# Activation codes turned as 16-bit halves, and the whole of attention's first score pass beside layer 1's tail, in a four-layer kernel on one core

## Chip, core and metric

One core of a Trainium2 chip runs one fixed program. The metric is device time in microseconds (us) of one execution, taken as the median of the runs. TensorE is called PE in the profile, VectorE DVE, ScalarE ACT, GpSimd POOL, and SyncE (which issues the DMAs) SP.

## What is computed

Eight batches of 512 tokens by 256 features pass through four layers, with modulations made from a conditioning vector. Layer 0 is a gated recurrence and an MLP whose activations are rounded to 8-bit codes before every product; layer 1 blends a style in and has a gelu MLP; layer 2 is attention with 16 heads; layer 3 a state-space layer and an MLP. Cut to the two parts that the change touches:

```python
# layer 0: every linear step, 7 products with wi, wf, wg, wo, wm1 (two halves), wm2
def _act_quant(x):
    scale = 127.0 / clip(max(abs(x), axis=-1), 1e-05)
    return clip(round(x * scale), -128, 127) / scale
def _bitlinear(x, w, nw):
    xn = x * rsqrt(mean(square(x), -1) + 1e-08) * nw
    return _act_quant(xn) @ _weight_quant(w).T

# layer 2: q, k, v of 16 heads of 16 features, with rotary positions
attn = einsum('bhnd,bhmd->bhnm', q, k) * scale
attn = softmax(attn, axis=-1)
out = einsum('bhnm,bhmd->bhnd', attn, v)
```

## The kernel before

The tokens of a batch lie in T = 4 tiles of 128 (one token per partition). All products need the features on the partitions, so tiles are turned on PE through an identity matrix (`turn`, L94) into PSUM and copied from there by ACT or DVE. PSUM has eight banks of 128 x 512 float32.

The program has three blocks of time. A setup runs to about 85 us. The block `layers01` runs layers 0 and 1 over the eight batches to 887.72 us in the profiled execution, where all engines meet; then `layers23` runs attention in rounds, and at its end layer 3.

The order within `layers01` is written by hand. Each engine has a table (`PE_TURN`, `DVE_TURN`, `ACT_TURN`, `POOL_TURN`, `SP_TURN`) of steps (stage, tile, batches ahead), which is gone through once per batch, so that up to five batches are in work at once. A second set of tables (`PE_BESIDE` and so on) hangs steps of attention's batch 0 behind named steps of the last batches of layer 1; B - 1 is the last batch. What stands in those tables is left out of the tables of attention. An engine executes its list strictly in order; signals (semaphores) between engines say when an item may start.

**Codes of layer 0.** ACT multiplies a tile by its scale and adds ROUND = 12582912.0, so that float32 rounding leaves the integer code in the lowest bits of the number: stages `xq` (L1167, three tiles of 256 features per token tile), `xoq` (L1190), `xq2` (L1198), `hq` (L1215). PE turns the float32 values through `ident`: 24, 8, 8 and 32 turns of 128 x 128 in a batch, 72 in all. DVE reads the bank, subtracts ROUND and writes bf16: `qT` (L1523, 128 x 768 over two banks), `qoT` (L1553, 128 x 256), `qT2` (L1594, 128 x 512), `qhT` (L1621, 128 x 512). The 768 columns of `xq` fill bank 0 and half of bank 1. Bank 1 is also read by ACT's gate step (L1175, signal `sg_ready`), so `xq` of a tile waits for that of the tile before. The products follow as `proj` (L88).

**Scores of attention.** A score pass over one batch has 64 rows (16 heads x 4 query tiles): PE computes a 128 x 512 row (stage `s`, L2158), DVE takes its maximum (L2194). After 16 rows the maxima of four heads are split into three bf16 parts (`npart`, L2201 to L2205), turned on PE (`nturn`, L94), copied (`nkeep`, L2210) and laid by three DMAs of SP (L1941) into three extra rows of q. The matching rows of k hold ones, which POOL sets by a memset of 3 x 8192 (L1957, step `ones`). The second score pass (`st`, L2035) then gives scores less their maximum, for ACT to exponentiate (L1983), and `pv` (L2044) multiplies by v. From batch 1 on, q and k are copied early by ACT (L2018) and laid out by 24 DMAs of SP (L1935, `dup`); the first score row of a batch waits for all of them.

Of batch 0, rows 0 to 47 stand beside the end of layer 1, over banks 0 and 1, two or three rows behind each `f1` or `f2` step (the gelu MLP's products, L88 and L1461); rows 48 to 63 stand in the middle of attention's first round. PE issues row n once DVE has reduced row n - 2.

Of the kernel before, what the change touches and what calls it, by code (L numbers as in the profile page):

```python
# [618 lines left out]
SP_BESIDE = ((("dup", 0, 0), ("dup", 1, 0), ("nkeep", 0, 0)), (("nkeep", 1, 0),))  # L619
# [39 lines left out]
    ("f1", 5, B - 1): (("s", 21, 0), ("s", 22, 0)),
    ("f1", 6, B - 1): (("s", 23, 0), ("s", 24, 0), ("s", 25, 0)),  # L660
    ("f1", 7, B - 1): (("s", 26, 0), ("s", 27, 0)),
    ("f2", 0, B - 1): (("s", 28, 0), ("s", 29, 0), ("s", 30, 0)),
    ("f2", 1, B - 1): (("s", 31, 0), ("s", 32, 0)),
    ("f2", 2, B - 1): (("s", 33, 0), ("s", 34, 0), ("s", 35, 0)),
    ("f2", 3, B - 1): (("s", 36, 0), ("s", 37, 0), ("nturn", 1, 0)),
    ("f2", 4, B - 1): (("s", 38, 0), ("s", 39, 0), ("s", 40, 0)),
    ("f2", 5, B - 1): (("s", 41, 0), ("s", 42, 0)),
# [2092 lines left out]
```

## Time and profile before

| | us |
|---|---|
| runs | 1993.22, 1990.77, 1985.62 |
| median | 1990.77 |
| the profiled execution | 1985.53 |
| its span (first to last instruction of the profile) | 1983.7 |
| PE busy in the span | 1747.9 (88%) |
| DVE busy | 1359.0 (69%) |
| ACT busy | 1106.3 (56%) |
| POOL busy | 615.3 (31%) |

The profiled execution is 1.8 us longer than its span. "Busy" counts an engine while one of its instructions runs; matmuls overlap, so pitches (start to start) say more about PE than durations. PEclk is the clock granted to PE as a share of full speed, 2.4 GHz; the lower level is 1.2 GHz. A time in a list of instructions is the start, then the duration of the whole group, with the count behind it. Text in brackets is how long the engine had been idle, and what it waited for.

### The profile page before, as it was taken

How to read it: one execution, taken by the hardware profiler on the slowest of the kernel's cores; microseconds unless marked ns; L12 is line 12 of the kernel's file. 1: busy time of each engine (PE TensorE's matmuls, PEld its weight loads, DVE VectorE, ACT ScalarE, POOL GpSimd, SP SyncE). 2: the span in 40 equal slices, each digit the busy share in tenths (PEclk: the TensorE clock that was granted, in tenths of full speed). 3: DMA queues.
4: the chain of work that ended last, by engine and by line, in shares of the span. 5: the costliest groups of instructions: out<-in, count | busy, mean ns of one | idle time of the engine just before them, and what ended most of it. 6: DMA issues, size and time to landing. Idle time of an engine off the chain costs nothing.

```text
span 1983.7 us, 25674 instructions
## 1 busy us (share of the span) xinstructions
PE 1747.9 (88%) x8444; PEld 1046.9 (53%) x8463; DVE 1359.0 (69%) x2873; ACT 1106.3 (56%) x2117; POOL 615.3 (31%) x874
## 2 busy tenths in 40 slices
PE   1367677989999999878989999999999998999998
PEld 1145455667667657543344444454545444666666
DVE  5755888888887765567867686877686734566650
ACT  6634667868867753314675757566666664322221
POOL 0145556756754633620000001010101012334342
PEclk9756788999999999988999999999999999999999
DMA  9440000000000002303030303030303005000000
GB/s 373 123 158 1 10 19 20 12 9 19 14 1 14 20 4 65 65 17 64 5 67 5 67 5 67 5 67 4 67 4 67 4 4 149 3 11 22 11 22 21
DMA packets 94422, 83.57 MB, mean 42 GB/s; under 512 B 9881, under 2 KB 87842, under 8 KB 94034
## 3 DMA queue, kind: packets, MB, share of 16 engines
q1 hardware_dynamic: 94192, 81.91, 15.1%
q8 instruction: 68, 1.11, 0.2%
q14 instruction: 64, 0.52, 0.1%
q10 hardware_dynamic: 98, 0.03, 0.0%
HBM read 51.26 MB, written 5.09 MB: 28 GB/s over the span
## 4 chain that ended last, share of the span: by engine, by line
PE 40%; DVE 8%; ACT 6%; issue 1%; POOL 0%; POOLq 0%; DVEq 0%; ACTq 0%
PE k_psum L88 13%; PE k_psum L2518 6%; PE k_psum L2044 5%; PE k_psum L2105 5%; PE k_psum L2158 5%; PE k_psum L2035 4%; PE k_psum L94 3%; DVE l_small L2194 2%; ACT l_prob L1983 1%; ACT L1983 1%; ACT L1999 1%; ACT l_gu L1999 1%; DVE l_xn L2267 1%; DVE l_small L2181 1%; DVE l_xn L2269 1%
## 5 line engine op out<-in xcount | busy, mean ns | idle before, releaser
L2194 DVE TENSOR_REDUCE l_small<-k_psum 128x1 f32<-128x512 f32 x512 | 329.7, 685 | 134.9 <-PE k_psum L2158 131.5
L1983 ACT ACTIVATE l_prob<-k_psum 128x512 f32<-128x512 f32 x512 | 286.4, 596 | 184.5 <-PE k_psum L2035 181.3
L1971 POOL TENSOR_TENSOR k_x_res<-k_x_res,k_arena_a 128x256 f32<-128x256 f32 x32 | 23.2, 726 | 418.5 <-DVE k_arena_a L2238 418.5
L2044 PE MATMUL k_psum<-l_prob,l_v 128*32 128x512 f32 x1024 | 138.1, 612 | 0.2
L2105 PE MATMUL k_psum<-k_arena_a,l_gu 128*128 128x256 f32 x512 | 135.6, 394 | 0.7 <-ACT l_gu L1999 0.7
L88 PE MATMUL k_psum<-l_turned_over,k_arena_a 128*128 128x512 f32 x256 | 120.8, 596 | 4.2 <-ACT l_gu L1999 4.2
L88 PE MATMUL k_psum<-k_arena_b,l_w_f 128*128 128x512 f32 x256 | 122.0, 604 | 0.0
L1461 PE MATMUL k_psum<-l_w_f,k_arena_b 128*128 128x256 f32 x512 | 120.4, 380 | 0.2 <-ACT k_arena_b L1274 0.2
L88 PE MATMUL k_psum<-l_hT,k_arena_b 128*128 128x512 f32 x256 | 114.3, 593 | 0.0
L2518 PE MATMUL k_psum<-k_arena_b,l_gu 128*128 128x256 f32 x512 | 113.0, 379 | 0.0
L2105 PEld LDWEIGHTS k_psum<-k_arena_a,l_gu 128*128 128x128 f32 x512 | 98.1, 198 | 19.7 <-issue 2.2
L2463 ACT ACTIVATE l_gu<-k_psum,k_arena_c 128x512 f32<-128x512 f32 x64 | 44.0, 687 | 112.3 <-PE k_psum L88 112.3
L2518 PEld LDWEIGHTS k_psum<-k_arena_b,l_gu 128*128 128x128 f32 x512 | 96.9, 190 | 16.1 <-issue 3.8
L2158 PE MATMUL k_psum<-l_kT,l_qT 96*128 96x512 bf16 x256 | 90.8, 397 | 15.7 <-DVE l_small L2194 14.2
L1461 PEld LDWEIGHTS k_psum<-l_w_f,k_arena_b 128*128 128x128 f32 x512 | 94.4, 190 | 13.3 <-ACT k_arena_b L1274 0.7
L2035 PE MATMUL k_psum<-l_qT,l_kT 99*128 99x512 bf16 x256 | 88.6, 391 | 12.6 <-PEq L2702 5.9
L2035 PE MATMUL k_psum<-k_arena_b 99*128 99x512 bf16 x256 | 87.4, 385 | 10.2 <-ACT l_prob L1983 9.2
L88 PE MATMUL k_psum<-k_t_wm,l_qT 128*128 128x512 bf16 x237 | 75.3, 420 | 22.9 <-DVE k_arena_a L1601 13.9
L2158 PE MATMUL k_psum<-k_arena_b 96*128 96x512 bf16 x256 | 90.8, 394 | 3.2 <-DVE l_small L2194 1.6
L94 PE MATMUL k_psum<-k_ident,k_arena_a 128*128 128x128 f32 x451 | 71.0, 296 | 24.4 <-ACT k_arena_c L1175 14.8
L88 PE MATMUL k_psum<-k_arena_a,l_xT 128*128 128x512 f32 (+1 forms) x256 | 89.4, 493 | 0.4 <-DVE l_xn L2255 0.4
L2579 DVE TENSOR_TENSOR l_add<-k_psum,k_arena_c 128x256 f32<-128x256 f32 x32 | 13.6, 424 | 96.7 <-PE k_psum L2518 96.7
(389 smaller groups left out, 3873.4 us busy)
## 6 DMA issues: line engine op xcount, KB each, us to landing
su_raw<-in_L_cond_wa SPq DMA_DIRECT2D x6, 1536.0 KB, 21.8
k_arena_b<-k_arena_c SPq DMA_DIRECT2D x32, 192.0 KB, 3.5
k_x_res<-in_x SPq DMA_DIRECT2D x1, 4096.0 KB, 19.9
k_arena_b<-k_arena_c SPq DMA_DIRECT2D x32, 128.0 KB, 3.2
out<-k_x_res SPq DMA_DIRECT2D x8, 512.0 KB, 2.9
l_mod_mlp<-mod SPq DMA_DIRECT2D x8, 384.0 KB, 3.6
l_qT<-k_arena_c SPq DMA_DIRECT2D x16, 192.0 KB, 3.6
l_kT<-k_arena_c SPq DMA_DIRECT2D x16, 192.0 KB, 3.3
```

Of the source, the lines that this page charges most:

```text
L88: last = nc.tensor.matmul(out, w, m, start=(i == 0), stop=(i == len(pairs) - 1), **kw)
L94: return nc.tensor.matmul(out, in_, ident, is_transpose=True, start=True, stop=True)
L1461: last = pe.matmul(psum[:, 6 + i % 2, 0:D], gu[:, f, tok(i)], w_f2[:, f, :], start=(f == 0), stop=(f == KF - 1))
L1983: act.activation(prob[:, s % 2, j, :], psum[:, 2 + n % 2, :], ACT.Exp, scale=float(HD) ** -0.5).then_inc(exp_ready.sem, 1)
L1999: act.activation(gu[:, n, :], psum[:, 5 + n % 2, :], ACT.Gelu).then_inc(gu_ready.sem, 1)
L2035: pe.matmul(psum[:, 2 + n % 2, :], kT[e % 2][:, head, tok(s % T)], qT[e % 2][:, head, :], start=True, stop=True).then_inc(st_ready.sem, 1)
L2044: last = pe.matmul(psum[j * BLOCK:(j + 1) * BLOCK, 4, :], v[e % 2][:, kt, at:at + BLOCK], prob[:, n % 2, j, :], start=(kt == 0), stop=(kt ...
L2105: last = pe.matmul(psum[:, mlp_bank(e, t), 0:D], gu[:, f, tok(t)], w_2[:, f, :], start=(f == 0), stop=(f == KF - 1))
L2158: pe.matmul(psum[:, n % 2, :], qT[e % 2][0:SROWS, n // T, tok(n % T)], kT[e % 2][0:SROWS, n // T, :], start=True, stop=True).then_inc(s_re ...
L2194: dve.tensor_reduce(mx[:, n % T, n // T:n // T + 1], psum[:, n % 2, :], AX.X, ALU.max).then_inc(max_ready.sem, 1)
L2463: act.activation(gu[:, n, :], psum[:, n % 2, :], ACT.Gelu_apprx_tanh, bias=b_1[:, n:n + 1]).then_inc(gu_ready.sem, 1)
L2518: last = pe.matmul(psum[:, 2 + n % 2, 0:D], gu[:, f, tok(n)], w_2[:, f, :], start=(f == 0), stop=(f == KF - 1))
```

## The change

1. **Codes as halves.** ACT adds ROUND + 0x4380 (17280) in place of ROUND, so the lower 16 bits of the float32 number are themselves a valid, positive bf16 pattern. PE turns only these lower halves, as bf16 values with a step of two elements, through the upper halves of `ident` (also with a step of two), and writes bf16 into the bank. DVE reads them as unsigned 16-bit integers and subtracts 17280. All 72 turns of a batch change. The 768 columns of `xq` now fit bank 0, and its wait for `sg_ready` goes.
2. **Scores.** All 64 rows of batch 0 and all four groups of maxima stand beside the end of layer 1, over banks 0, 1 and 4: up to four rows behind each step. PE issues row n of batch 0 once row n - 3 is reduced. SP issues the DMAs of groups 2 and 3 before the block's end.
3. **Ones.** Those of batch 0 are written by ACT (an exponential with scale 0 over 3 x 8192) behind the last gelu step. Those of batch 1 are cut into eight memsets of POOL.

```diff
+MIDDLE = 0x4380
-    ("s5p", 4, B - 1): (("ones", 0, 0),),
+    ("gelu", 7, B - 1): (("ones", 0, 0),)}
-SP_BESIDE = ((("dup", 0, 0), ("dup", 1, 0), ("nkeep", 0, 0)), (("nkeep", 1, 0),))
+SP_BESIDE = ((("dup", 0, 0), ("dup", 1, 0), ("nkeep", 0, 0)), (("nkeep", 1, 0), ("nkeep", 2, 0), ("nkeep", 3, 0)))
 # PE_BESIDE, two of its lines
-    ("f1", 2, B - 1): (("s", 13, 0), ("s", 14, 0), ("s", 15, 0)),
+    ("f1", 2, B - 1): (("s", 19, 0), ("s", 20, 0), ("s", 21, 0), ("s", 22, 0)),
...
+        def low(a, cols):
+            return a.bitcast(BF16).rearrange("p (n a) -> p n a", a=2)[:, cols, 0]
+        identh = ident[:].bitcast(BF16).rearrange("p (n a) -> p n a", a=2)[:, :, 1]
+        def halves(a):
+            return psum[:, a, :].bitcast(BF16)
+        def codes(a):
+            return psum[:, a, :].bitcast(U16)
...
-   last = ac.activation(xw[:, t, j, :], xw[:, t, j, :], ACT.Copy, bias=ROUND, scale=qs[e % 2][:, t, j:j + 1])
+   last = ac.activation(xw[:, t, j, :], xw[:, t, j, :], ACT.Copy, bias=ROUND + MIDDLE, scale=qs[e % 2][:, t, j:j + 1])
...
                             pe.wait_ge(qT_ready.sem, qT_ready.at(e, t))
-                            pe.wait_ge(sg_ready.sem, sg_ready.at(e, t))
...
-   last = turn(nc, two_banks(0)[:, tok(j)], xw[:, t, j // KD, tok(j % KD)], ident[:])
+   last = turn(nc, halves(0)[:, tok(j)], low(xw[:, t, j // KD, :], tok(j % KD)), identh[:])
...
-   V.tensor_scalar(qT[...], two_banks(0)[:, 0:3 * D], ROUND, None, ALU.subtract)
+   V.tensor_scalar(qT[...], codes(0)[:, 0:3 * D], float(MIDDLE), None, ALU.subtract)
    # xoq/qoT, xq2/qT2 and hq/qhT in the same way
...
+    def banks_of(e, n):
+        return (0, 1) if e else (0, 1, 4)
+    def s_bank(e, n):
+        return banks_of(e, n)[n % len(banks_of(e, n))]
     def max_bank(e, n):
-        return 5 if e == 0 and n < 2 else 7
+        return 7 if e else 5
...
-                if n >= 2:
-                    pe.wait_ge(max_ready.sem, max_ready.at(e, n - 1))
+                if n >= len(banks_of(e, n)):
+                    pe.wait_ge(max_ready.sem, max_ready.at(e, n - len(banks_of(e, n)) + 1))
...
-                if e:
-                    pool_chain.link(nc.gpsimd.memset(v[1][:], 1.0))
-                nc.gpsimd.memset(kT[e][SROWS:SROWS + MROWS, :, :], 1.0).then_inc(ones_ready, 1)
+                pool_chain.link(nc.gpsimd.memset(v[1][:], 1.0))
+                for h in range(0, HEADS, 2):
+                    nc.gpsimd.memset(kT[1][SROWS:SROWS + MROWS, h:h + 2, :], 1.0).then_inc(ones_ready, 1)
...
+            if stage == "ones":
+                act.activation(kT[0][SROWS:SROWS + MROWS, :, :].rearrange("p h n -> p (h n)"),
+                               ident[SROWS:SROWS + MROWS, 0:1].to_broadcast([MROWS, HEADS * L]),
+                               ACT.Exp, scale=0.0).then_inc(ones_ready, 1)
```

**PE, steps f1 2 to f1 5 of layer 1's last batch.** L88 on `k_arena_b,l_w_f` is an f1 step, L2158 the score rows, L94 on `l_npart` a turn of maxima. Before:

```order
L88 MATMUL k_psum<-k_arena_b,l_w_f 128x512 x2
L2158 MATMUL k_psum<-l_kT,l_qT 128x512 x3
L88 MATMUL k_psum<-k_arena_b,l_w_f 128x512 x2
L2158 MATMUL k_psum<-l_kT,l_qT 128x512 x2
L88 MATMUL k_psum<-k_arena_b,l_w_f 128x512 x2
L2158 MATMUL k_psum<-l_kT,l_qT 128x512 x3
L94 MATMUL k_psum<-l_identb,l_npart 12x128 x4
```

Now (the score rows are L2181, the products L91, the turns L97):

```order
L91 MATMUL k_psum<-k_arena_b,l_w_f 128x512 x2
L2181 MATMUL k_psum<-l_kT,l_qT 128x512 x4
L97 MATMUL k_psum<-l_identb,l_npart 12x128 x4
L91 MATMUL k_psum<-k_arena_b,l_w_f 128x512 x2
L2181 MATMUL k_psum<-l_kT,l_qT 128x512 x4
```

Each step is followed by four rows, and the first turn of maxima stands one step earlier.

**PE, the middle of attention's first round.** L2158 on `l_kT,l_qT` are rows 48 to 63 of batch 0, L2158 on `k_arena_b` the rows of batch 1, L2035 and L2044 the second pass and its product with v. Before:

```order
L94 MATMUL k_psum<-l_identb,l_part 96x128 x8
L2035 MATMUL k_psum<-l_qT,l_kT 128x512 x2
L2158 MATMUL k_psum<-l_kT,l_qT 128x512 x10
L2044 MATMUL k_psum<-l_prob,l_v 32x512 x4
L2158 MATMUL k_psum<-l_kT,l_qT 128x512
L2035 MATMUL k_psum<-l_qT,l_kT 128x512
L2158 MATMUL k_psum<-l_kT,l_qT 128x512 x5
L2035 MATMUL k_psum<-l_qT,l_kT 128x512 x2
L2158 MATMUL k_psum<-k_arena_b 128x512 x2
```

Now:

```order
L97 MATMUL k_psum<-l_identb,l_part 96x128 x8
L2058 MATMUL k_psum<-l_qT,l_kT 128x512 x2
L2067 MATMUL k_psum<-l_prob,l_v 32x512 x4
L2058 MATMUL k_psum<-l_qT,l_kT 128x512 x3
L2181 MATMUL k_psum<-k_arena_b 128x512 x2
```

The sixteen rows are gone from here, and the first rows of batch 1 stand right behind the last turns of q and k.

**ACT, the end of the block.** The last gelu steps are L1274, and L1983 is attention's exponential. Before:

```order
L1274 ACTIVATE k_arena_b<-k_psum,l_small 128x512 x8
L867 UNCONDITIONAL_BRANCH
L2606 UNCONDITIONAL_BRANCH
L1983 ACT_TABLE_LOAD
L1983 ACTIVATE l_prob<-k_psum 128x512
```

Now:

```order
L1287 ACTIVATE k_arena_b<-k_psum,l_small 128x512 x8
L1998 ACT_TABLE_LOAD
L1998 ACTIVATE l_kT<-k_ident 3x8192
L880 UNCONDITIONAL_BRANCH
L2631 UNCONDITIONAL_BRANCH
L2006 ACTIVATE l_prob<-k_psum 128x512
```

The ones stand in front of the block's end, and with them the load of the exponential's table.

## Rows read from the trace of the kernel before

**Rows 1.** All engines by stretch: start:end, length, busy (count), PEclk, DMA share, GB/s
```profile
95.00:232.00 137.00, 84.48 (x355) 57.40 (x356) 82.15 (x173) 61.70 (x172) 69.61 (x95) 0.61 0.21 69
232.00:350.00 118.00, 87.73 (x484) 64.33 (x486) 101.42 (x211) 83.17 (x218) 70.67 (x97) 0.83 0.06 17
...
524.00:610.00 86.00, 82.45 (x458) 60.36 (x460) 74.03 (x151) 68.24 (x165) 50.42 (x68) 0.98 0.03 9
...
820.00:888.00 68.00, 49.72 (x181) 28.06 (x180) 47.04 (x85) 5.78 (x9) 26.71 (x39) 0.92 0.03 12
```

**Rows 2.** PE's longest wait from 524 to 610: total us, times, longest
```profile
PE k_psum L88 <- DVE k_arena_a L1601: 2.0, 2, 1.1
```

**Rows 3.** PE's turns by group, 350 to 820: shapes, count, busy us, mean ns
```profile
L94 PE MATMUL k_psum<-k_ident,k_arena_a 128*128 128x128 f32 x288 | 40.5, 273 | 1.9 <-ACT k_arena_c L1175 1.4 <-DVE l_add L1627 0.5
L94 PE MATMUL k_psum<-k_ident,k_arena_c 128*128 128x128 f32 x112 | 17.7, 273 | 0.1
```

**Rows 4.** PE in order of time: float32 turns, then bf16 turns (start, duration)
```profile
744.21 0.60 PE L94 MATMUL k_psum<-k_ident,k_arena_a 128*128 128x128 f32 x4
744.64 0.60 PE L94 MATMUL k_psum<-k_ident,l_xn 128*128 128x128 f32 x4
...
779.46 0.61 PE L94 MATMUL k_psum<-l_identb,l_part 128*96 128x128 bf16 x8
```

**Rows 5.** DVE by group: reading codes (350 to 820), bf16 maxima (830 to 888)
```profile
L1621 DVE TENSOR_SCALAR l_qhT<-k_psum 128x512 bf16<-128x512 f32 x48 | 32.2, 684 | 4.3 <-PE k_psum L94 4.3
...
L1523 DVE TENSOR_SCALAR l_qT<-k_psum 128x768 bf16<-128x768 f32 x16 | 15.3, 954 | 12.9 <-PE k_psum L94 12.9
...
L2210 DVE COPY k_max_rows<-k_psum 12x512 bf16<-12x512 bf16 x2 | 0.8, 401 | 0.0
```

**Rows 6.** PE, and one row of DVE, in order of time, layer 0 of batch 0
```profile
120.60 1.52 PE L94 MATMUL k_psum<-k_ident,k_arena_a 128*128 128x128 f32 x6 [1.39 <-ACT k_arena_c L1175]
...
126.02 1.51 PE L94 MATMUL k_psum<-k_ident,k_arena_a 128*128 128x128 f32 x6 [1.38 <-ACT k_arena_c L1175]
...
122.15 0.96 DVE L1523 TENSOR_SCALAR l_qT<-k_psum 128x768 bf16<-128x768 f32 x1 [1.14 <-PE k_psum L94]
```

**Rows 7.** PE's wait for the gate step, 232 to 350
```profile
PE k_psum L94 <- ACT k_arena_c L1175: 4.7, 4, 2.3
```

**Rows 8.** PE in order of time, the end of layer 1, and DVE's last row there
```profile
828.62 1.88 PE L88 MATMUL k_psum<-k_arena_b,l_w_f 128*128 128x512 f32 x4
...
831.50 0.39 PE L2158 MATMUL k_psum<-l_kT,l_qT 96*128 96x512 bf16 x1 [0.57 <-DVE l_small L2194]
831.73 1.88 PE L88 MATMUL k_psum<-k_arena_b,l_w_f 128*128 128x512 f32 x4
...
847.65 1.21 PE L2158 MATMUL k_psum<-l_kT,l_qT 96*128 96x512 bf16 x2 [6.62 <-DVE l_small L2194]
...
881.40 0.60 PE L2158 MATMUL k_psum<-l_kT,l_qT 96*128 96x512 bf16 x2
...
884.77 1.38 DVE L2189 TENSOR_SCALAR l_xn<-k_x_res,l_small 128x256 f32<-128x256 f32 x4
```

**Rows 9.** POOL, then DVE, in order of time, at the ones of batch 0
```profile
837.87 6.92 POOL L1957 MEMSET l_kT<- 3x8192 bf16 x1
...
837.94 6.88 DVE L2201 TENSOR_SCALAR l_npart<-l_small 128x16 bf16<-128x16 f32 x1
```

**Rows 10.** ACT in order of time, its first instruction of attention
```profile
887.72 1.28 ACT L1983 ACT_TABLE_LOAD   x1 [28.09 <-PEq L2702]
```

**Rows 11.** PE in order of time, the middle of attention's first round
```profile
921.01 0.60 PE L2158 MATMUL k_psum<-l_kT,l_qT 96*128 96x512 bf16 x2 [0.52 <-ACT k_arena_c L2018]
...
934.49 1.01 PE L2158 MATMUL k_psum<-k_arena_b 96*128 96x512 bf16 x2
```

**Rows 12.** SP's queue in order of time, and DMA busy tenths, 905 to 935 in 40 slices
```profile
910.02 19.20 SPq L1935 DMA_DIRECT2D k_arena_b<-k_arena_c  x24
...
DMA  0000000048889998737975087999998898810000
```

More of the change, by code:

```diff
@@ L17 @@
 BF16 = mybir.dt.bfloat16
+U16 = mybir.dt.uint16
 B, L, D = 8, 512, 256
@@ L659 @@
[L659 to L667, printed above, removed]
@@ L670 @@
+    ("f2", 1, B - 1): (("s", 47, 0), ("s", 48, 0), ("s", 49, 0), ("s", 50, 0)),
+    ("f2", 2, B - 1): (("s", 51, 0), ("s", 52, 0), ("s", 53, 0), ("s", 54, 0)),
+    ("f2", 3, B - 1): (("s", 55, 0), ("s", 56, 0), ("s", 57, 0), ("s", 58, 0), ("nturn", 2, 0)),
+    ("f2", 4, B - 1): (("s", 59, 0), ("s", 60, 0), ("s", 61, 0), ("s", 62, 0)),
+    ("f2", 5, B - 1): (("s", 63, 0),),
+    ("f2", 7, B - 1): (("nturn", 3, 0),)}
 DVE_BESIDE = {
@@ L1321, in _ @@
                         for k in range(KD):
-                            last = turn(nc, psum[:, t % 2, tok(k)], xo[:, t, tok(k)], ident[:])
+                            last = turn(nc, halves(t % 2)[:, tok(k)], low(xo[:, t, :], tok(k)), identh[:])
                         last.then_inc(xo_turned.sem, 1)
@@ L1337, in _ @@
                             for k in range(KD):
-                                last = turn(nc, psum[:, 4 + t, tok(KD * i + k)], mx2[:, 2 * t + i, tok(k)], ident[:])
+                                last = turn(nc, halves(4 + t)[:, tok(KD * i + k)], low(mx2[:, 2 * t + i, :], tok(k)), identh[:])
                         last.then_inc(turned2.sem, 1)
@@ L1355, in _ @@
                         for k in range(T):
-                            last = turn(nc, psum[:, 4 + (3 * i + c) % 2, tok(k)], h[:, i, tok(c * T + k)], ident[:])
+                            last = turn(nc, halves(4 + (3 * i + c) % 2)[:, tok(k)], low(h[:, i, :], tok(c * T + k)), identh[:])
                         last.then_inc(h_turned.sem, 1)
@@ L2164, in pe @@
                     pe.wait_ge(nT_ready.sem, nT_ready.at(e, n))
-                front = e + 1 if n == NG - 1 else e
+                front = e + 1 if n == NG - 1 and e else e
                 pe.wait_ge(v_ready.sem, v_ready.at(min(front, B - 1), T))
-                if n == 2 and e + 1 < B:
+                if n == 2 and 0 < e < B - 1:
                     pe.wait_ge(xT_ready.sem, xT_ready.at(e + 1, KD))
@@ L2587, in turns @@
         for b in range(B + 1):
-            yield from attention_order(b)
+            for item in attention_order(b):
+                if item not in EARLY2:
+                    yield item
     def late(table):
```

69 lines of the change are left out of this document (36 added, 33 removed).

## The prediction

> **What bounds the kernel now.** I read the stretches first, then who waits for whom in each. In the steady part of layers 0 and 1 PE is busy 82.45 of 86 us at a clock of 0.98, DVE 74.03, ACT 68.24, POOL 50.42 [rows 1]; the longest sum of PE's waits there is 2.0 us [rows 2]. PE sets the pace, and DVE is not far behind. From 95 to 232 no engine is busy for more than 85 of 137 us and PE's clock is 0.61: chains of steps set the time, and each wait on them counts whole. From 232 to 350 DVE is the busiest, 101.42 of 118, and PE waits 4.7 us for the gate step [rows 1, 7]. At the end of layer 1 the score rows run through PE and DVE together, PE busy 49.72 and DVE 47.04 of 68: a slot of two f1 products and three rows takes 831.73 - 828.62 = 3.11 us, because the third row waits 0.57 for the reduction that frees its bank, and one stall of 6.62 stands in it [rows 1, 8]. From 888 on, attention's rounds follow one another; the change shortens only the first of them.
>
> **PE's turns, steady part.** Four float32 turns take 744.64 - 744.21 = 0.43 us from start to next start, about 109 ns each. From first start to last end the four take 0.60, and eight bf16 turns 0.61 [rows 4]: half as long each, about 55 ns. If a turn of halves goes like bf16, it saves 53 ns. From 350 to 820 the 288 turns of `k_arena_a` are codes (`xq`, `hq`), and 16 of every 24 of `k_arena_c` are (`xoq` and `xq2`, beside 8 plain ones), 75 of 112 [rows 3]: 363 in all, and 576 - 363 = 213 before 350. 363 x 53 ns = 19.2 us. The bf16 rows read packed values, and nothing in the trace reads every second one, so the saving lies between 0 (a read of 16 bits in 32 goes like float32, the 109 ns row) and 53; below 0 it would go only if the step cost more than the float32 that fills the same bytes, for which no row speaks. I take 53, since these are bf16 matmuls of the same shape but for the step. Of 19.2 I keep 16.5: PE has 3.55 us of slack in 86 now, and with 3.8 less work a batch the chains through DVE and ACT are waited for a little more often.
>
> The Trainium skill ("SBUF — State Buffer", on its cachelines) says that a step is free as long as at least two accesses fall into a 16-byte line, up to 8 bf16 elements; a step of two lies inside that. By it the saving is the 53 ns; by the pessimistic end it is nothing. No run here has shown it yet.
>
> **DVE's readings.** 128 x 512 float32 takes 684 ns and 128 x 768 takes 954; a bf16 copy of 512 columns out of PSUM takes 401 [rows 5]. A reading of 16-bit integers lies between 401 and 684. I take 410 for 512 columns and 540 for 768, nearest to the bf16 copy. That is about 5 us per batch off DVE (8 readings of `hq` at 0.27, 4 of `xq` at 0.41, 2 of `xq2`, 4 of `xoq` at 0.14). In the steady part this is off the path and worth nothing by itself, but it keeps DVE behind PE: 74.03 less 5.8 in 86 is 68.2, against PE's 82.45 less 4.4 = 78.0. It matters where the chains are bare, at the start.
>
> The Trainium skill ("VectorE: DVE Perf Modes", Why PSUM operands drop a tier) puts a PSUM operand at most at the double rate, and float32 from PSUM at the single; with the row of 401 ns the trace agrees for bf16. If subtraction from integers stayed at the single rate, the start would give 3.3 us less (8 tiles x 0.41).
>
> **The start, 95 to 350.** In batch 0 a tile takes 126.02 - 120.60 = 5.42 us: the gate wait 1.38, six turns at the half clock, the reading, the product. The gate wait goes, the turns lose 6 x 107 = 0.64 (half clock, twice 53), the reading 0.41: 2.4 us, if PE alone decided. But DVE waits only 1.14 per tile [rows 6] and does its list in order, so a tile can shrink by about 1.14 + 0.41 = 1.5. With the first tile not gaining the wait, batch 0 gives about 4.9. In batch 1 the tiles are also held by ACT's and POOL's chain of the batch ahead; I take 1.9, and 0.5 for the other turns up to 232. From 232 to 350 some 140 turns are worth 140 x 53 = 7.4 and the gate waits 4.7 [rows 7], together 12 at the most; DVE, the busiest there, loses about 7 of its 101. I take 5, with 2 and 9 as ends. Start in all: 12.3, between 6 and 18.
>
> **The end of layer 1.** Four rows over three banks: three go out at once, the fourth waits for one reduction, as the third of three does over two banks, so I price the slot again at 3.11 us. Without its wait a slot of three rows takes 3.11 - 0.57 = 2.5, with two rows 0.39 less, 2.2. From 820.0, where the first row starts: 2.2, 3 slots of three rows at 2.5 (three banks, no wait), 13 of four at 3.11, then 2.0 + 1.8 + 1.8 for the last three steps and 1.8 for the turns of maxima and three of layer 1's own: 57.5, so the last f2 ends at 877.5 where it now ends near 881.4 [rows 8]. The 6.62 stall came from POOL's memset of 6.92 us, beside which one small DVE instruction took 6.88 [rows 9]; it is gone, and pays for the sixteen rows that are added. Its follow-on, a step at the half clock, goes too. Behind it now stand DVE's last steps to 886.15 and the engines' meeting, 1.6 to 887.72 [rows 8, 10]. After, the meeting waits for three DMA issues of SP instead (19.20 / 24 = 0.8 each, rows 12), 2.4, since nturn 3 and its copy run beside DVE's last steps: 877.5 + 2.4 + 1.6 = 881.5 in place of 887.72, **6.2 us**, with 3 (the issues start only once DVE has done everything) and 8 as ends. The ones on ACT: POOL writes the same 3 x 8192 in 6.92 us [rows 9], and even at twice that they are hidden, as ACT idles 28.09 us there [rows 10]. If that cover were gone, they would cost their 7 to 14 us whole. The 1.28 of the table load moves under the same cover, though round 0's turns wait for other things as well, so I count nothing for it.
>
> **The first round.** Sixteen rows leave the middle, from 921.01 to about 933.4 [rows 11]. But what follows them, the first row of batch 1, needs all 24 `dup` DMAs: SP issues them until 910.02 + 19.20 = 929.22, and the queues are busy up to slice 35 of 40, about 932 [rows 12]. So a wait for DMA takes the place of the rows, and of 13 us at the most I count 934.49 - 932.4 = **2.1**, with 0 and 3.3 (the last issue at 929.22 plus 2) as ends; no row shows when the last of the 24 lands, only that the queues are empty then. The memset of batch 1 in eight pieces costs seven more instruction starts, which ACT's copy of v waits for; I charge 0.3 as an estimate, 0 to 1 as ends.
>
> **The sum.** 12.3 + 16.5 + 6.2 + 2.1 - 0.3 = 36.8 us. From the profiled execution, 1985.53 - 36.8 = 1948.7. The median of the runs stands 5.2 above that execution, and from it the sum gives 1954.0. I predict between them, **1952**.
>
> **The rivals.**
> (a) *The step costs what float32 costs.* PE's 16.5 goes, and about 4 at the start (1.3 in batch 0 where DVE decides, the rest from 232 to 350); gate wait, DVE, the end and the first round stay: 36.8 - 20.5 = 16.3; from 1988.2, midway between the two starting points, about 1972. For it: the bytes passed over are the same. Against: the bf16 rows. By the page on SBUF it would not happen.
> (b) *Another engine becomes the bound.* ACT at 68.24 and DVE at 68.2 of 86 are in chains with PE; if only half of PE's 19.2 arrives, and half of the 12.3: 36.8 - 6.9 - 6.1 = 23.8, about 1964.
> (c) *More arrives than I count* (all of 19.2, 16 at the start): 43.2, about 1945.
> (d) *Slower: PE's clock falls.* From 232 to 350, with the same steps but more waits, the granted clock is 0.83, against 0.98 [rows 1]. If shorter turns open enough gaps that the steady part runs at 0.83 too, PE's 78.0 us in 86 become 78.0 x 0.98 / 0.83 = 92.1, 6.1 more than 86; over the 470 us from 350 to 820 that is +33, where +16.5 of gain was counted: the sum is 36.8 - 16.5 - 33 = -12.7, about 2001. It decides where the steady part loses the 20.3 that the rest gains, 3.7 us in 86: 78.0 x 0.98 / 89.7, a clock of 0.85. Against it: PE would still be busy nine tenths of the time.
> (e) *The halves are not read faster by DVE either*: 3.3 less, 1955; inside the forecast's own range.
>
> **Chances.** Forecast with (e), 1945 to 1960: 0.58. (a) 0.14, (b) 0.16, (c) 0.08, (d) 0.04. The range leaves out (d) and the outer part of (c) and (a): **1938 to 1973**. A measurement of this kernel can tell about 0.5% (10 us) from no change; the forecast, (a), (b) and (c) lie beyond that, (a) least clearly. Faster 0.93, same 0.04, slower 0.03.
>
> **What would show it.** In the profile after: eight turns of codes in about 0.45 us (if four take 0.43, (a)); readings at 410 and 540 ns; tiles of batch 0 at 3.9 us and no wait for L1175's successor; PEclk above 0.95 from 350 on (else (d)); slots of 3.1 us at the end of layer 1 with no stall over 1 us, and 61.5 us (now 67.7) from the first score row to attention's start; PE waiting for a DMA, 8 us or so, before batch 1's first row, with that row only 2 us nearer to the round's start. Wrong it would be above all if the turns' 53 ns is not there, or if that DMA wait is longer than the rows it replaces.

## The result, and the profile after

The changed kernel took 1970.95 us in the median of four runs (1969.29 to 1973.95), beside 1991.99 for the kernel before (its three runs and a fourth of 1993.38): a ratio of 0.9902, with a 95% interval of 0.9877 to 0.9928. Over all ten executions of it (six more stood in the last series of experiments) the median is 1969.6. The profiled execution took 1969.29 us, 16.2 less than that of before. The prediction's 1952 was 19 us too low: faster, as forecast, by about half of what was forecast.

The stretches of the kernel after (start:end, length, busy and count of PE, PEld, DVE, ACT, POOL, PEclk, DMA share, GB/s), which answer to [rows 1]:

```profile
232.00:350.00 118.00, 82.54 (x482) 56.98 (x481) 94.31 (x206) 83.20 (x226) 73.82 (x99) 0.84 0.05 17
...
524.00:610.00 86.00, 81.67 (x458) 59.80 (x457) 61.12 (x135) 67.06 (x165) 52.02 (x72) 0.94 0.05 16
...
820.00:888.00 68.00, 53.21 (x203) 28.08 (x203) 46.39 (x104) 19.89 (x21) 16.52 (x22) 0.92 0.04 13
```

DVE is down from 74.03 to 61.12 busy in the same 86 us, but PE's clock there is 0.94 and no longer 0.98. That stretch shows more of the fall than the steady part as a whole, where the clock went from 0.97 to 0.96. The whole of it from 350 to 820, after and then before:

```profile
350.00:820.00 470.00, 446.70 (x2322) 311.16 (x2320) 327.28 (x718) 317.18 (x732) 261.82 (x407) 0.96 0.09 24
350.00:820.00 470.00, 449.41 (x2286) 321.62 (x2300) 352.60 (x715) 323.07 (x750) 256.50 (x390) 0.97 0.09 24
```

PE's longest waits from 524 to 610 (total, times, longest), which answer to [rows 2]:

```profile
PE k_psum L97 <- ACT l_xn L1253: 2.9, 1, 2.9
PE k_psum L91 <- DVE k_arena_a L1613: 1.1, 2, 0.9
```

A wait for the first `xn` of layer 1, which is 0.6 us long before, has grown to 2.9. The line of before, in the same stretch:

```profile
548.43 0.66 PE L94 MATMUL k_psum<-k_ident,l_xn 128*128 128x128 f32 x4 [0.61 <-ACT l_xn L1240]
```

The operations themselves came out as priced. PE in order of time, six turns of codes; then DVE's readings from 350 to 820 by group:

```profile
533.28 0.51 PE L97 MATMUL k_psum<-k_ident,k_arena_a 128*128 128x128 bf16 x6
533.63 1.94 PE L1473 MATMUL k_psum<-l_w_f,k_arena_b 128*128 128x256 f32 x8
```

```profile
L1633 DVE TENSOR_SCALAR l_qhT<-k_psum 128x512 bf16<-128x512 uint16 x48 | 19.4, 417 | 4.1 <-PE k_psum L97 4.1
L1535 DVE TENSOR_SCALAR l_qT<-k_psum 128x768 bf16<-128x768 uint16 x16 | 8.8, 552 | 13.8 <-PE k_psum L97 13.8
```

Six turns in 533.63 - 533.28 = 0.35 us are 58 ns each (109 before, 56 forecast), so reading every second 16-bit element costs PE next to nothing (packed bf16: about 55). The readings take 417 and 552 ns (forecast 410 and 540).

Where the 16.2 us came from, by marks that both traces have:

| mark | before | after | gained so far |
|---|---|---|---|
| first xn of layer 1 turned | 255.74 | 248.01 | 7.7 |
| turn of layer 1's second norm (`yn`), batch 1 | 387.59 | 377.24 | 10.4 |
| first xn of layer 1 turned, two batches on | 399.50 | 390.95 | 8.6 |
| first score row | 820.03 | 806.58 | 13.5 |
| start of attention (turn of its first xn) | 888.29 | 872.67 | 15.6 |
| first score row of batch 1 | 934.49 | 918.33 | 16.2 |
| end | 1983.7 | 1967.5 | 16.2 |

The end of layer 1 gave 2.2 (forecast 6.2) and the first round 0.5 (1.8). How the rest is shared depends on the mark: with the mark in front of the steady part's first long wait for `xn` the start has 10.4 (forecast 12.3) and the steady part 3.1 (16.5); with the mark just behind that wait it is 8.6 and 4.9. Either way twelve to thirteen of the twenty missing microseconds are in the steady part. These are two single executions, and the start scatters by itself: the first `xn` begins on ACT at 252.4 to 257.9 us in the four traces with float32 turns, and at 245.0 to 250.0 in the eleven with the turns, waits and POOL order of after up to there.

### The profile page after: what moved, and what is told of

The parts are those of the page before. It is cut to its first block, busy times and chain, and to the rows that moved or that the text cites. A ratio compares the mean times of both kernels' runs of the same rounds, so it can differ in the third digit from the quotient of the medians.

```text
span 1967.5 us, 25698 instructions
## 1 busy us (share of the span) xinstructions
PE 1719.6 (87%) x8463; PEld 1017.9 (52%) x8463; DVE 1310.6 (67%) x2873; ACT 1112.7 (57%) x2118; POOL 611.8 (31%) x880
## 4 chain that ended last, share of the span: by engine, by line
PE 40%; DVE 8%; ACT 6%; issue 1%; SPq 0%; DMA 0%; POOL 0%; POOLq 0%; DVEq 0%; ACTq 0%
PE k_psum L91 13%; PE k_psum L2541 6%; PE k_psum L2067 5%; PE k_psum L2128 5%; PE k_psum L2181 4%; PE k_psum L2058 4%; PE k_psum L97 3%; ACT l_prob L2006 1%; DVE l_small L2217 1%; ACT L2006 1%; ACT L2022 1%; ACT l_gu L2022 1%; DVE l_xn L2290 1%; DVE l_small L2204 1%; DVE l_xn L2292 1%
## 5 line engine op out<-in xcount | busy, mean ns | idle before, releaser
L91 PE MATMUL k_psum<-l_turned_over,k_arena_a 128*128 128x512 f32 x256 | 120.9, 596 | 4.2 <-ACT l_gu L2022 4.2
L91 PE MATMUL k_psum<-k_arena_b,l_w_f 128*128 128x512 f32 x256 | 120.4, 597 | 0.0
L91 PE MATMUL k_psum<-l_hT,k_arena_b 128*128 128x512 f32 x256 | 114.3, 592 | 0.0
L2181 PE MATMUL k_psum<-k_arena_b 96*128 96x512 bf16 x256 | 90.5, 393 | 8.6 <-DMA k_arena_b<-k_arena_c 5.7
L91 PE MATMUL k_psum<-k_t_wm,l_qT 128*128 128x512 bf16 x256 | 81.6, 432 | 17.4 <-DVE k_arena_a L1613 10.6
L2181 PE MATMUL k_psum<-l_kT,l_qT 96*128 96x512 bf16 x256 | 86.5, 387 | 8.3 <-DVE l_small L2217 7.0
L91 PE MATMUL k_psum<-k_arena_a,l_xT 128*128 128x512 f32 (+1 forms) x256 | 92.5, 506 | 0.4 <-DVE l_xn L2278 0.4
L2602 DVE TENSOR_TENSOR l_add<-k_psum,k_arena_c 128x256 f32<-128x256 f32 x32 | 13.5, 423 | 96.6 <-PE k_psum L2541 96.6
L1219 ACT ACTIVATE k_arena_a<-k_psum,l_small 128x512 f32<-128x512 f32 x64 | 43.9, 686 | 55.7 <-PE k_psum L91 55.6
```

The lines of the kernel that those rows point to most:

```text
L91: last = nc.tensor.matmul(out, w, m, start=(i == 0), stop=(i == len(pairs) - 1), **kw)
L1219: ac.activation(h[:, t // 2, t % 2 * 512:(t % 2 + 1) * 512], psum[:, 4, :], ACT.Silu, scale=deq2[:, t // 2:t // 2 + 1]).then_inc(sgate_rea ...
L2181: pe.matmul(psum[:, s_bank(e, n), :], qT[e % 2][0:SROWS, n // T, tok(n % T)], kT[e % 2][0:SROWS, n // T, :], start=True, stop=True).then_i ...
```

## Experiments

### Each half of the change alone

`x1_codes` is the kernel before with the codes as halves and nothing else; `x2_scores` the kernel after with the codes as float32, over two banks and with the wait for the gate step.

```diff
# x1_codes, against before: every hunk of part 1 of the change, as
-   turn(nc, psum[:, t % 2, tok(k)], xo[:, t, tok(k)], ident[:])
+   turn(nc, halves(t % 2)[:, tok(k)], low(xo[:, t, :], tok(k)), identh[:])
```

> The kernel before with the codes turned as halves and nothing else of the change. Theory T1 (from the traces of before and after): in the steady part the stretch of a batch from the first xoq to the first xn of layer 1 lasts as long as ACT's and POOL's in-order lists (22.7 us before, 23.0 after), so the 50 of 72 turns that lie in it save nothing; about 10.4 us are won up to 350 and 3 in the steady part, so 13 us in all, 1972 to 1975 in the profiled execution. Rival T2 (the halves take the steady part's saving back through PE's clock, wherever the turns lie) gives the same total, but then PE's wait for xn stays under 1 us a batch. Rival T3 (the score part costs something that hides the codes' gain): this kernel gains 25 or more.

> The kernel after with the codes turned as float32, through two banks and with the wait for the gate step, as before; the score part of the change stays. The traces give 2.2 us at the end of layer 1 and 0.5 in attention's first round: 2 to 3 us less than before, 1983. If the parts help or hinder each other (T3), it is not the complement of the kernel with codes alone: then faster by 6 or more, or slower.

Measured: `x1_codes` 1972.32 us (ratio to before 0.9937, 0.9916 to 0.9957), `x2_scores` 1986.07 (0.9998, 0.9984 to 1.0012). The codes carry most of the gain: 14.9 us between the medians of that series, where the whole change has 19 to 21 in other series, and the intervals of the two ratios overlap. The score part can't be told from nothing in the runs (1 us between the medians, 2 to 3 expected); its trace shows the same 2.2 us at layer 1's end as the whole change (68.26 from the first score row to attention's start before, 66.06 here, 66.09 after). T3 falls. PE waits 2.9 us and more for `xn`, as T1 says and not under 1 us, T2's sign. But what T2 says of the clock is there as well: from 350 to 800 the half-clock stretches add up to 44.4 us in `x1_codes`, 37.5 in after, and 27.3 before.

### Is it PE that paces the stretch before xn?

`x3_root3` changes the order on POOL alone. `x5_pe` and `x7_pe3` make the turns of `xq` two and three times from batch 3 on, `x9_before_pe` makes them twice in the kernel before. (T4, in two of the expectations, is the theory that PE's long wait for `xn` is followed by stretches at the half clock, which cost more than extra turns do.)

```diff
# x3_root3, against after (POOL_TURN)
-    ("x2", 2, 2), ("xb", 1, 0), ("xb", 2, 0), ("root2", 0, 3), ("x2", 3, 2), ("mx", 3, 5), ("root3", 0, 2), ("sgn", 0, 4), ("xb", 3, 0),
+    ("x2", 2, 2), ("xb", 1, 0), ("root2", 0, 3), ("x2", 3, 2), ("root3", 0, 2), ("xb", 2, 0), ("mx", 3, 5), ("sgn", 0, 4), ("xb", 3, 0),
# x5_pe, against after (x7_pe3: the first range twice; x9_before_pe: the same line of before)
-                        for j in range(3 * KD):
+                        for j in [*range(3 * KD if e >= 3 else 0), *range(3 * KD)]:
```

> The kernel after with one change of order on POOL: root3 (which the first xn of layer 1 waits for) ahead of xb 2 and mx 3, and root2 ahead of xb 2. If T1 holds, xn starts 1 to 2 us earlier in each batch and PE's wait of 2.9 for it shrinks by as much: 4 to 5 batches in the steady part, so 5 to 9 us less than after, and a steady period of 72 us in place of 73.5. If PE's own work or its clock is the bound (T2), the period stays within 0.3 us and the time within 2.

> The kernel after with each of the 24 turns of xq made twice from batch 3 on (the second overwrites the first with the same values): 24 x 56 ns = 1.3 us more PE work a batch, nearly all inside the stretch that T1 says PE doesn't pace. T1: PE's wait for xn falls from 2.9 to about 1.6 us and the period doesn't change, within 0.3 us (under 2 us in all). T2: the period grows by 1.3 us, 6 to 7 us in all over five batches.

> The kernel after with the turns of xq made three times from batch 3 on: 2.6 us more PE work a batch. T4: PE's wait for xn goes to about 0.5 us, the half clock stands only behind the 32 one-column products, and the period is 72.3 to 73 us (the extra work is still covered by the stretch that ACT and POOL pace): 1957 to 1962. If more PE work simply costs its time: 6.5 us above the kernel with the turns made twice, 1965.

> A control: the kernel before with its 24 float32 turns of xq made twice from batch 3 on, 2.6 us more PE work a batch. Before has only 0.6 us of wait for xn to fill, so if what counts is the wait that is filled (T4), this is slower by about 2 us a batch, 8 to 10 us in all. If extra turns help by themselves, wherever they stand, it is faster than before.

Measured: `x3_root3` 1971.19 us, no better than after, where T1 expected 5 to 9 less and T2 no change; `x5_pe` 1958.69 in one run, twelve less than after although it only adds work, which neither theory expected; `x7_pe3` 1969.60 in one, above both figures of its expectation; `x9_before_pe` 1993.33 in one, against 1986.5 for before beside it, 6.8 slower where 8 to 10 were expected. Single runs decide little here, since one kernel scatters by ten to twelve us (below). To read them I took from each trace, for the three batches from 365 to 590, how long it is from ACT's first `xoq` to its first `xn`, and how long to the next `xoq`:

| kernel | xoq to xn, us | turns of codes in it | whole period, us | PE's wait at xn |
|---|---|---|---|---|
| before | 22.7, 22.8, 22.7 | 50 | 74.7, 74.3, 73.4 | 0.6 |
| x9_before_pe | 22.9, 22.9, 22.9 | 56 | 74.9, 74.7, 74.4 | 0.0 |
| after | 23.2, 23.0, 23.0 | 50 | 74.4, 73.3, 74.8 | 3.0, 2.9, 2.9 |
| x1_codes | 23.2, 23.0, 23.0 | 50 | 76.1, 75.1, 75.1 | 3.0, 2.9, 2.9 |
| x5_pe | 22.6, 22.6, 22.6 | 68 | 72.4, 72.3, 72.3 | 1.8 |
| x7_pe3 | 22.6, 22.6, 22.6 | 86 | 72.8, 74.8, 72.8 | 0.9 to 1.0 |
| x3_root3 | 20.6, 20.6, 20.6 | 50 | 74.9, 74.9, 74.6 | 0.5 |

Fifty of a batch's 72 turns of codes stand between these marks, and the stretch is as long with 50 bf16 turns as with 86, or with 50 in float32. PE does not pace it: of what those 50 save (50 x 53 ns = 2.65 us), 2.3 comes back as the wait at `xn`, which goes from 0.6 to 2.9. What does pace it is shown by `x3_root3`: with root3 earlier on POOL the stretch is 2.4 us shorter. POOL in order of time, kernel after, and ACT's `xn` behind it:

```profile
458.67 0.72 POOL L1053 TENSOR_TENSOR k_x_res<-k_x_res,l_add 128x256 f32<-128x256 f32 x1
459.35 0.72 POOL L1001 TENSOR_TENSOR k_arena_c<-k_arena_c,l_mod_norm 128x256 f32<-128x256 f32 x1
460.15 0.73 POOL L1002 TENSOR_TENSOR k_arena_c<-k_arena_c,l_mod_norm 128x256 f32<-128x256 f32 x1
460.97 0.20 POOL L978 TENSOR_SCALAR l_small<-l_small 128x4 f32<-128x4 f32 x1
461.25 1.60 POOL L979 TENSOR_TENSOR l_small<-l_small 128x4 f32<-128x4 f32 x1
...
462.88 0.51 ACT L1253 ACTIVATE l_xn<-k_x_res,l_small 128x256 f32<-128x256 f32 x1 [1.07 <-POOL l_small L979]
```

root3 is L978 and L979; the two instructions of `mx` (L1001, L1002) stand in front of it. But the batch is not shorter in `x3_root3`. The wait has only moved on by one link, from `xn` to the copy of `xT` on ACT. PE in order of time there:

```profile
464.18 0.66 PE L97 MATMUL k_psum<-k_ident,l_xn 128*128 128x128 f32 x4 [0.48 <-ACT l_xn L1253]
...
469.37 0.63 PE L97 MATMUL k_psum<-k_ident,l_xn 128*128 128x128 f32 x4 [2.16 <-ACT k_arena_b L1260]
469.84 0.51 PE L97 MATMUL k_psum<-k_ident,k_arena_a 128*128 128x128 bf16 x6
470.19 3.40 PE L1473 MATMUL k_psum<-l_w_f,k_arena_b 128*128 128x256 f32 x8
```

The last row shows the second half of the story: these eight products take 3.40 us, where they take 1.9 at the full clock. And the period goes with the half clock rather than with the stretch. In the thirty batches of the ten kernels that have the halves, one-column dots and no instruction added on ACT, it is 71.8 to 72.8 us where 3.4 us of the batch are at the half clock (16 batches), 73.2 to 74.8 with 6.8 (4), and 74.6 to 76.1 with 10.2 (10).

### ACT or POOL?

`x4_act` puts one more instruction on ACT in front of the gate step of tile 1.

```diff
+                        if e >= 4 and t == 1:
+                            act.wait_ge(ssqh_ready.sem, ssqh_ready.at(e - 2, T))
+                            ac.activation(junk_h[:], ident[:, 0:1].to_broadcast([P, FF]), ACT.Copy).then_inc(extra_done, 1)
... # and a wait of ACT's next write to junk_h for extra_done
```

> The kernel after with one more instruction on ACT in batches 4 to 7, in front of the gate step of tile 1 (it writes scratch that nothing reads; 128 x 1024, about 1.0 us). T1 (from the first xoq to the first xn the stretch goes at ACT's and POOL's pace): the stretch grows from 23.0 to 24 us where the instruction stands in it, PE's wait for xn from 2.9 to 3.9. If PE paced it, the stretch would not change.

Measured: 1980.92 us in one run, and the stretch is 23.2, 23.0, 23.0 us, not 24. That expectation failed. The added 1.04 us went into the 1.07 for which ACT waits for root3 anyway, so of "ACT's and POOL's lists" it is POOL's that ends the stretch. The ten us by which the run is above after lie elsewhere. Almost six stand in front of the first added instruction (392.1 us): the fourth batch's `xoq` is at 371.4 us against 365.5, where both kernels are the same. The rest is in the periods, 75.5, 76.9 and 75.2, with 6.8 to 10.2 us at the half clock in each.

### What the wait does to the clock

PE of the kernel after in order of time, around the wait at `xn` in the next batch, and the stretches there (columns as above):

```profile
538.43 0.66 PE L97 MATMUL k_psum<-k_ident,l_xn 128*128 128x128 f32 x4 [2.86 <-ACT l_xn L1253]
538.93 1.37 PE L91 MATMUL k_psum<-k_t_ifg,l_qT 128*128 128x256 bf16 x6
540.09 3.07 PE L1473 MATMUL k_psum<-l_w_f,k_arena_b 128*128 128x256 f32 x8
```

```profile
535.60:539.00 3.40, 0.57 (x5) 0.56 (x6) 1.62 (x3) 2.19 (x5) 3.32 (x5) 1.00 0.00 0
539.00:542.40 3.40, 3.40 (x13) 2.70 (x12) 1.29 (x2) 2.97 (x9) 3.24 (x6) 0.51 0.00 0
542.40:546.00 3.60, 3.60 (x27) 3.12 (x26) 1.76 (x5) 2.15 (x8) 1.31 (x3) 0.99 0.02 5
```

In the first of these PE works 0.57 of 3.40 us; in the second it works all the time, at the lower of its two levels (1.2 GHz), which costs 3.4 / 2 = 1.7 us of work. The other place of a batch with half-clock stretches is at the end of the 32 one-column products of the dots, or right behind them: so in 38 of 42 batches. The expectation of `x11_wide` says that it was so in every trace, which is not right: one batch of before and the three of `x4_act` have none there. `x11_wide`, `x13_wide64` and `x12_before_wide` widen those products.

```diff
# x11_wide and x12_before_wide: WD = 32, x13_wide64: WD = 64
-   mm(nc, psum[:, 3, i:i + 1], [(g[:, k, tok(i)], styleT[:, k, e:e + 1]) for k in range(KD)])
+   mm(nc, psum[:, 3, WD * i:WD * i + WD], [(g[:, k, tok(i)], styleT[:, k, e:e + 1].to_broadcast([P, WD])) for k in range(KD)])
... # the dots of gsq in the same way; DVE reads every WD-th column
```

> The kernel after with the 32 one-column products of the dots widened to 32 equal columns each (the operand is one column read again; DVE reads one column of each). The same weights are loaded, and each product still hides behind the next load (142 ns each), so PE's list takes no longer. In every trace so far a stretch at the half clock of 3.4 or 6.8 us follows these products. Theory T5: the clock falls because the products are so thin, not because of what the change did. Then these stretches go, worth 1.7 to 3.4 us a batch over seven batches, 12 to 20 us: 1950 to 1958. If the clock falls for another reason (its being weight loads that wait, or the time of the batch), the stretches stay and the time is within 3 us of after.

> The kernel before with the same widening to 32 columns. T5: it gains as well, 8 to 15 us (1972 to 1979), since before has half-clock stretches of 3.4 to 6.8 us at the same place; then the difference between the two kernels with wide products shows what the change is worth with the clock out of the way: 13 to 20 us. If the products are not the reason, within 3 us of before.

> As the kernel after with 32 equal columns, but 64: 107 ns of columns behind a load of 142 ns. T5 with the width: if 32 columns remove the half-clock stretches only in part, 64 remove more of them; if 32 remove all, the same time as with 32; if PE's columns begin to show in the list, 1 us a batch slower.

Measured: 1971.05 us (0.9913, 0.9897 to 0.9930), 1985.28 (0.9997, 0.9986 to 1.0008) and, in one run, 1965.24. T5 had 12 to 20 us and 8 to 15: it is mostly right about the place and wrong about the price. The half clock at the dots goes in eight of the nine batches (in the first of `x11_wide` it stays), and the medians win nothing; the 1965.24 is a single run. PE of `x12_before_wide` in order of time:

```profile
501.46 0.59 PE L89 MATMUL k_psum<-k_t_wm,l_qT 128*128 128x512 bf16 x2
504.77 0.59 PE L89 MATMUL k_psum<-k_t_wm,l_qT 128*128 128x512 bf16 x2 [2.71 <-DVE k_arena_a L1602]
...
507.75 3.08 PE L89 MATMUL k_psum<-k_arena_b,l_w_f 128*128 128x512 f32 x4
```

Behind the dots DVE has a chain of its own (6.4 us from the dots' end to the reading that PE waits for), and PE at the full clock only waits longer for it: 2.71 us in place of 1.4 or less. In most batches the wait ends 7.2 to 7.3 us behind the dots' end, whatever the clock. The work behind that wait then goes at the half clock (four products 3.08 us, 1.88 otherwise). This is a second stretch that PE doesn't pace, and the same give-back. The kernel before does it too, in the one batch whose dots were not followed by the half clock:

```profile
428.59 0.59 PE L88 MATMUL k_psum<-k_t_wm,l_qT 128*128 128x512 bf16 x2 [2.71 <-DVE k_arena_a L1601]
...
431.57 2.80 PE L88 MATMUL k_psum<-k_arena_b,l_w_f 128*128 128x512 f32 x4
```

Over all the traces of this study, three batches of each, a wait of 2.8 us or more at `xn` was followed by 3.4 us at the half clock in 14 of 18 batches, and the wait of 2.71 behind the dots by 3.4 or 6.8 in each of the 12 batches that have it. No wait of 1.8 us or less at `xn` was followed by one, in 30 batches (those of `x3_root3` left out, where the wait of 2.05 to 2.16 stands one link on and was followed by one each time). But short waits are not safe as such. Behind the dots, a wait of 1.22 to 1.53 us with one of 0.93 close behind it was followed by 3.4 us at the half clock in four batches (of `x1_codes`, `x7_pe3`, `x11_wide` and `x17_after`); with a first wait of 1.20 or less it was not. PE of `x1_codes` in order of time:

```profile
420.51 0.59 PE L91 MATMUL k_psum<-k_t_wm,l_qT 128*128 128x512 bf16 x2 [1.36 <-DVE k_arena_a L1612]
...
422.69 1.01 PE L91 MATMUL k_psum<-k_t_wm,l_qT 128*128 128x512 bf16 x2 [0.93 <-DVE k_arena_a L1612]
423.50 3.16 PE L91 MATMUL k_psum<-k_arena_b,l_w_f 128*128 128x512 f32 x4
```

### The idle time in pieces

That is correlation; the next kernels change only how the idle time lies. `x6_sg` puts the wait of `xq` for the gate step back, `x14_sg3` does so from batch 3 on.

```diff
# x14_sg3, against after
                             pe.wait_ge(qT_ready.sem, qT_ready.at(e, t))
+                            if e >= 3:
+                                pe.wait_ge(sg_ready.sem, sg_ready.at(e, t))
```

> The kernel after with the wait of xq for the gate step put back. The prediction put most of the start's gain there: 1.38 us in each of three tiles of batch 0 and in batch 1. If that is right, the first xn of layer 1 (245.8 us after, 253.5 before) comes 3 to 5 us later, at 249 to 251; the steady part does not change, since no wait for the gate step stands in it. If the shorter turns and readings made the start's gain, it stays within 1 us of 245.8.

> The kernel after with the wait of xq for the gate step put back from batch 3 on only. Theory T6: the steady period does not hang on how much PE idles but on how long at a stretch: a wait of 2.9 us at xn is mostly followed by 3.4 us at the half clock, which costs 1.7 us a batch, while the same idle time in pieces (three waits for the gate step and 0.3 at xn, as with the wait in all batches) is not. Then xn waits 0.3, the period is 72.0 to 72.5 in place of 73.3 to 74.8, and with the start of after (first xn at 246) the whole is 6 to 9 us less than after. If an added wait can't help (T2), it is the same as after or slower.

> The changed kernel again, beside the other two on the same chip: 1969 to 1974, as at first. Its steady periods show whether the stretches at the half clock behind the wait for xn come back in another execution: T6 expects one in at least two batches of three, and a period of 74 to 75 us where it stands and 73.3 where not.

Measured: `x6_sg` 1968.30 us in one run; `x14_sg3` 1966.34 (six runs, 1960.57 to 1970.79; 0.9889, 0.9871 to 0.9908); the kernel after beside it (`x17_after`) 1967.98 (six, 1962.69 to 1972.47; 0.9903, 0.9886 to 0.9920), just under the 1969 expected.

| kernel | xoq to xn | period | wait at xn | half clock behind it |
|---|---|---|---|---|
| x17_after | 23.2, 23.0, 23.0 | 76.0, 74.8, 74.6 | 3.0, 2.9, 2.9 | 3 of 3 |
| x6_sg | 22.4, 22.4, 22.4 | 72.5, 72.0, 72.3 | 0.3 | 0 of 3 |
| x14_sg3 | 22.4, 22.4, 22.4 | 72.4, 72.5, 73.2 | 0.3 | 0 of 3 |

PE's waits of `x14_sg3` from 380 to 660, against 8.8 us in three waits for `xn` after:

```profile
PE k_psum L97 <- ACT k_arena_c L1188: 6.8, 6, 1.8
PE k_psum L91 <- DVE k_arena_a L1615: 4.7, 5, 1.1
...
PE k_psum L97 <- ACT l_xn L1253: 0.9, 3, 0.3
```

An added wait that takes no work away makes the period 1 to 4 us shorter. It breaks one long idle time into pieces of 1.8 us and less, and no half clock follows `xn`. That it is the clock that counts, and not the wait, can be seen where the clock is alike, though in one batch of each: the one batch of after whose wait of 2.86 was not followed by the half clock takes 73.3 us, and the batch of `x14_sg3` with as much half clock (6.8 us) 73.2. So the steady part of the profiled executions shows T6 as expected. In the medians it is not shown: 1966.3 against 1968.0 lies inside a scatter of ten us within each kernel, and between the profiled executions (1966.73 and 1972.47) it is 5.7 us, not quite the 6 to 9 of the expectation. Nor did `x6_sg` settle how much of the start's gain was the wait for the gate step: its first `xn` is at 247.9, between the two forecasts of its expectation, and inside the 245.0 to 250.0 of executions without that wait up to there.

### The end of layer 1, and a version that beats both

DVE of the kernel after in order of time, then SP's queue:

```profile
860.41 0.41 DVE L2233 COPY k_max_rows<-k_psum 12x512 bf16<-12x512 bf16 x1 [2.30 <-DMA l_qT<-k_max_rows]
...
866.21 1.38 DVE L2212 TENSOR_SCALAR l_xn<-k_x_res,l_small 128x256 f32<-128x256 f32 x4
867.50 0.42 DVE L1755 TENSOR_TENSOR k_x_res<-k_psum,k_x_res 128x256 f32<-128x256 f32 x1
867.84 0.40 DVE L2233 COPY k_max_rows<-k_psum 12x512 bf16<-12x512 bf16 x1
```

```profile
856.39 0.97 SPq L965 DMA_DIRECT2D skip<-l_junk  x1
857.41 12.66 SPq L1960 DMA_DIRECT2D l_qT<-k_max_rows  x9
```

The copy of nkeep 2 waits 2.30 us for the DMAs of nkeep 1, which had been ready since 842 but stand in SP's queue behind stores of layer 3's preparation; and nkeep 3 is DVE's very last item, so that SP's last three issues run alone, to 870.07. `x10_pe_tail` (on `x5_pe`) and `x15_sg3_tail` (on `x14_sg3`) move these items.

```diff
# SP_BESIDE and DVE_BESIDE
-SP_BESIDE = ((("dup", 0, 0), ("dup", 1, 0), ("nkeep", 0, 0)), (("nkeep", 1, 0), ("nkeep", 2, 0), ("nkeep", 3, 0)))
+SP_BESIDE = ((("dup", 0, 0), ("dup", 1, 0), ("nkeep", 0, 0), ("nkeep", 1, 0)), (("nkeep", 2, 0), ("nkeep", 3, 0)))
-    ("x3", 2, B - 1): (("s", 63, 0), ("npart", 3, 0), ("xn", 0, 1)),
-    ("x3", 3, B - 1): (("nkeep", 3, 0),)}
+    ("x3", 2, B - 1): (("s", 63, 0), ("npart", 3, 0), ("nkeep", 3, 0), ("xn", 0, 1))}
```

> The kernel after with the 24 turns of xq made twice from batch 3 on, and with three items moved at layer 1's end: SP issues nkeep 1's DMAs before it waits for the state-space preparation, and DVE copies nkeep 3 before it writes batch 1's xn. Theory T4 (PE's wait of 2.9 us for xn is followed by stretches at the half clock, which cost more than the extra turns do): 10 to 13 us less than after from the turns, as in the look at them alone (1958.7). The moved items remove DVE's wait of 2.3 us for a DMA and some 1.5 us between the last f2 and the start of attention: 2.5 us more. Together 1955 to 1958. T2 (the earlier look was chance): within 3 us of after.

> The same with the three items moved at layer 1's end (nkeep 1's DMAs ahead of SP's wait for the state-space preparation, nkeep 3 ahead of batch 1's xn), which took 3.5 us off the stretch from the first score row to attention's start in an earlier kernel (66.1 to 62.5). T6: 3 to 4 us less than without them, 1957 to 1960 in the profiled execution.

Measured: from the first score row to attention's start 62.5 us in both traces, 3.5 less than after. `x10_pe_tail` took 1964.50 us (1956.97 to 1968.75; 0.9903, 0.9870 to 0.9936), where 1955 to 1958 were expected: with more runs the extra turns are no longer worth twelve us, so the single run of `x5_pe` probably fell at the low end of a scatter of twelve. `x15_sg3_tail` took **1960.92 us** (1957.97 to 1963.59), a ratio to before of 0.9867 (0.9850 to 0.9884), below both kernels. Its interval lies below that of after beside it (0.9886 to 0.9920) and overlaps a little with the first one (0.9877 to 0.9928). Its profiled execution, 1957.97, is as expected.

## Why the prediction was off, point by point

- **Turns and readings.** Right: 58 ns (56), 417 and 552 ns (410, 540). Rival (a) did not happen. The Trainium skill ("SBUF — State Buffer", on its cachelines) has a step within 8 bf16 elements as free, and for the step of two the trace agrees. That the total came out at 1970.95, beside the 1972 of rival (a) and inside the stated range, is chance: the turns were saved and the time was lost elsewhere.
- **"Of 19.2 I keep 16.5."** This is the step that failed. From PE's 82.45 busy of 86 us and its short waits it concluded that "PE sets the pace" through the whole batch. A wait of 0.6 us in the trace of before only said that PE came 0.6 us early to a point whose time POOL's list sets, and 50 of 72 turns stand ahead of that point. Of 3.8 us a batch, 2.65 could not be kept; the other 22 turns' 1.2 fits the periods where the clock is alike (3.4 us of half clock, at the dots: 73.4 before, 72.0 to 72.5 in `x6_sg` and `x14_sg3`), though these rest on one batch of before.
- **The clock.** Rival (d) had the mechanism, gaps that pull the clock down, at a size that did not come: from 350 to 820 PE's clock is 0.96 (0.97 before), above the 0.95 that the forecast asked for and far from 0.83. The half-clock stretches grew from 27.3 to 37.5 us, which is about 5 us of PE's work (half of the added 10.2), of the same size as what the saving of the 22 turns left over. The forecast's sum had no term for the clock. Rival (b) had the result in kind, half of the gain, with ACT and DVE named in place of POOL.
- **The start.** Near in sum (10.4, or 8.6 by the later mark, for 12.3), and how it is made up was not shown. Tiles of batch 0 take 3.56 us (121.90 to 125.46), 3.9 forecast.
- **The end of layer 1.** Most slots are as forecast, 3.11 us, and the last f2 ends 58.7 us after the first row (57.5). The term was mis-sized behind it: 2.2 in all where 6.2, or at least 3, were given. nkeep 3 does not run beside DVE's last steps but after them, and DVE's wait of 2.30 for a DMA was not foreseen. With these items moved (`x15_sg3_tail`) the stretch is 68.26 - 62.5 = 5.8 us shorter than before.
- **The first round.** The DMA wait that takes the place of the sixteen rows is there, 5.67 us ("8 or so"):

```profile
918.33 1.03 PE L2181 MATMUL k_psum<-k_arena_b 96*128 96x512 bf16 x2 [5.67 <-DMA k_arena_b<-k_arena_c]
```

  but it ends only 0.5 us nearer to the round's start, not 1.8. The first products of q, k and v took 4.51 us for eight, at the half clock, where before they took 2.75, and everything up to `dup` followed 2 us later.
- **The other forecasts.** The ones on ACT took 7.03 us and were hidden. Left open: what sets the period once the wait for `xn` is gone and the clock is up (72 us in `x5_pe`, `x6_sg` and `x10_pe_tail`); how the half-clock stretches fall in an execution that isn't profiled, and with them how many of the ten us of scatter are theirs.

## What to carry to other kernels

An engine at 95% in an in-order program need not set the pace: before counting a saving on it, find the next point where it waits for another engine, however short that wait is, and ask what sets the time of that point. Work saved ahead of such a point only lengthens the wait there, and on PE a wait of two to three microseconds in one piece can cost more than the work did. Where PE will be idle anyway, it can pay to spread the idle time; here that shortened the period in the traces, while the medians don't show it.

## What the runs showed of the hardware that was not expected

- A wait of PE of 2.05 to 3.04 us in one piece was followed by 3.4 us or more at 1.2 GHz in 29 of 33 batches, although PE was busy all through those (539.00 to 542.40 in after: 0.51 of full speed, 3.40 of 3.40 us busy). A wait of 1.81 us and less at `xn` was not, in 30 batches, but two close ones (1.22 to 1.53, then 0.93) were in four.
- 32 products with one column each have a half-clock stretch at their end or right behind it in 38 of 42 batches, with 32 or 64 equal columns each in one of nine. At the full clock the extra columns cost nothing to speak of: 3.63 us for the 32 products with one column, 3.65 with 32 (`x12_before_wide`), 3.68 with 64 (`x13_wide64`).
- The same program scatters by up to twelve us (1956.97 to 1968.75 for `x10_pe_tail`), which is most of what a change of this size moves.
